# All weight splits on VectorE, loads of x and of running sums from GpSimd's queue, LoRA columns in two buffers, another order in the last unit: a fused dense and NF4 layer pair in float32

## The reference

```python
base  = einsum('bsi,oi->bso', x, weight) + bias1
low   = einsum('bsi,bri->bsr', x, lora_a[adapter])       # rank 16, one adapter per batch row
delta = einsum('bsr,bor->bso', low, lora_b[adapter])
h     = base + scale[adapter] * delta
w2    = NF4[codes] * absmax        # 64 elements to a block, 2048 x 2048
out   = x + (einsum('bsd,od->bso', h, w2) + bias2)
```

## Time and profile before

| | |
|---|---|
| time, median of 3 runs | 2107.86 us (2107.43 to 2111.29) |
| the profiled execution | 2105.49 us, its span 2103.7 us |
| TensorE busy | 96% of the span |
| VectorE busy | 77% |
| ScalarE busy | 42% |
| GpSimd busy | 6% |
| mean granted clock of TensorE | 0.985 |
| DMA | 526 MB, 250 GB/s over the span |

### The profile page before, as it was taken

How to read it: one execution, slowest core, us unless ns; L and a number is a source line. 1 busy time by engine, 2 the same in 40 slices (tenths; PEclk the granted TensorE clock), 3 DMA queues, 4 the chain that set the end, 5 groups by cost and what they waited for, 6 DMA issues and landing times.

```text
span 2103.7 us, 29439 instructions
## 1 busy us (share of the span) xinstructions
PE 2016.7 (96%) x10880; PEld 1713.2 (81%) x10880; DVE 1610.5 (77%) x2377; ACT 883.8 (42%) x1417; POOL 118.9 (6%) x79
## 2 busy tenths in 40 slices
PE   4899999999999999989999999989999999998997
PEld 4788778788878777889989989989997887886876
DVE  8899879866996465575577787787778778778887
ACT  8655555554555332343442342243242234234332
POOL 5100000000000000000020020020002002002000
PEclk8999999999999999999999999999999999999999
DMA  9778878887888788856478677786877878877876
GB/s 283 244 239 263 256 250 259 254 253 244 264 266 252 244 264 275 256 190 218 166 262 269 217 263 257 250 282 210 271 259 231 275 253 261 260 234 242 279 257 231
DMA packets 406277, 526.14 MB, mean 250 GB/s; under 512 B 22992, under 2 KB 293024, under 8 KB 406008
## 3 DMA queue, kind: packets, MB, share of 16 engines
q1 hardware_dynamic: 402824, 513.23, 75.6%
q0 software_dynamic: 3312, 11.03, 1.6%
HBM read 336.47 MB, written 188.76 MB: 250 GB/s over the span
## 4 chain that ended last, share of the span: by engine, by line
PE 80%; DVE 8%; DMA 5%; issue 3%; SPq 2%; ACT 1%; DVEq 0%; ACTq 0%
PE big L1638 19%; PE big L1640 19%; PE big L1639 19%; PE big L1826 10%; PE big L1824 10%; PE big L1653 2%; DVE comb L1324 2%; DMA rq<-xc_d 1%; PE big L1634 1%; DMA xc_d<-rq 1%; DMA a_br<-a_sel_d 1%; DMA comb_raw<-wc_d 1%; DVE r_sb L1452 1%; DMA code_w<-in_L_ffn_codes_dram 1%; DVE xs L1374 1%
## 5 line engine op out<-in xcount | busy, mean ns | idle before, releaser
L1824 PE MATMUL big<-comb,xs 128*128 128x256 f32 x1920 | 468.9, 282 | 15.0 <-DVE r_sb L1452 13.8
L1638 PE MATMUL big<-wq,tile 128*128 128x512 f32 x1088 | 468.4, 431 | 1.2 <-DVE tile L1259 1.2
L1826 PE MATMUL big<-comb,xs 128*128 128x272 f32 (+1 forms) x1920 | 468.0, 286 | 0.0
L1640 PE MATMUL big<-wq,tile 128*128 128x512 f32 x1088 | 427.2, 393 | 0.0
L1639 PE MATMUL big<-wq,tile 128*128 128x512 f32 x1088 | 426.3, 392 | 0.0
L1824 PEld LDWEIGHTS big<-comb,xs 128*128 128x128 f32 x1920 | 363.9, 190 | 20.1 <-DVE comb L1324 14.7
L1826 PEld LDWEIGHTS big<-comb,xs 128*128 128x128 f32 x1920 | 363.9, 190 | 2.3
L1638 PE MATMUL big<-comb,xs 128*128 128x512 f32 x832 | 332.3, 399 | 21.5 <-DVE r_sb L1452 14.8
L1452 DVE TENSOR_TENSOR r_sb<-big,r_sb 128x512 f32<-128x512 f32 x328 | 225.6, 688 | 149.7 <-PE big L1640 98.5
L1640 PE MATMUL big<-comb,xs 128*128 128x512 f32 x832 | 330.6, 397 | 0.0
L1639 PE MATMUL big<-comb,xs 128*128 128x512 f32 x832 | 330.4, 397 | 0.0
(11 more groups left out here) (144 smaller groups left out, 2440.7 us busy)
## 6 DMA issues: line engine op xcount, KB each, us to landing
raw<-in_L_cond_weight_dram SPq DMA_DIRECT2D x128, 512.0 KB, 4.5
xg<-xc_d SPq DMA_DIRECT2D x112, 512.0 KB, 5.3
xc_d<-rq SPq DMA_DIRECT2D x26, 1792.0 KB, 7.6
r_sb<-m_d SPq DMA_DIRECT2D x80, 512.0 KB, 4.9
m_d<-r_sb SPq DMA_DIRECT2D x64, 512.0 KB, 6.1
wc_d<-cs SPq DMA_DIRECT2D x31, 896.0 KB, 4.9
tb<-wc_d SPq DMA_DIRECT2D x107, 256.0 KB, 5.0
x_nat<-in_x_dram SPq DMA_DIRECT2D x104, 256.0 KB, 4.0
```

The costliest lines, as they stand in the source:

```text
L1638: nc.tensor.matmul(out_ap, t_hi, m_hi, start=first, stop=False, skip_group_check=onto)
L1640: return nc.tensor.matmul(out_ap, t_lo, m_hi, start=False, stop=last, skip_group_check=onto)
L1824: nc.tensor.matmul(big[:, bank, 0:HW], x, w[:, 0:HW], start=begin, stop=end, skip_group_check=not opens)
L1826: ins = nc.tensor.matmul(big[:, bank + 1, 0:wide], x, w[:, HW:HW + wide], start=begin, stop=end, skip_group_check=not opens)
```

## The change

- `BY_GPSIMD` goes. All 14 halves of every stage are split by VectorE. `LO_STEPS` gets the four: half 10 beside half 9 at step 8 (k = 1 of a stage's first unit), 11 at step 9 (k = 2), 12 at step 10 (k = 3), 13 at step 11 (k = 4).
- `load_x` and `load_base` move from SP to a loop on GpSimd: wait until all lower parts of unit u's x are made, load x of u + 1, then (for u + 1 in 8 to 47) wait for the store of the sum that used the buffer and load the running sum. The first x stays on SP with a semaphore of its own.
- `a_b` and `a_br` get a second buffer; `load_a(u + 2)` moves to the top of unit u (from u = 1 on) and waits for the placing of unit u's columns.
- In the last unit all four LoRA pairs are multiplied behind k = 3 and k = 4, those of the second block first; that block's totals are loaded ahead into the freed x buffer (`total_end`); the final additions are made in three parts of each block and each part is stored as it is done.

```diff
-    BY_GPSIMD, ON_VECTOR = (A12, A22), 10
     def half_at(i, f, c):
-        n = halves_of(i).index((f, c)) + 1
-        if i and f in BY_GPSIMD:
-            return 4 * (i - 1) + n - ON_VECTOR
-        return 2 * NF + ON_VECTOR * (i - 1) + n if i else n
+        return 2 * NF * i + halves_of(i).index((f, c)) + 1
-    LO_STEPS = {-1: [0], 0: [1], 2: [2], 3: [3], 5: [4], 6: [5, 6], 7: [7, 8], 8: [9]}
+    LO_STEPS = {-1: [0], 0: [1], 2: [2], 3: [3], 5: [4], 6: [5, 6], 7: [7, 8], 8: [9, 10], 9: [11], 10: [12], 11: [13]}
+    TAIL = ((0, slice(0, 2)), (1, slice(1, 2)), (1, slice(0, 1)))
+    def pair_at(u, n):
+        m, t = divmod(n, 2)
+        return (1 - m, t) if u == NU - 1 else (m, t)
+        total_end = at("total_end", 176, [P, 2, 2, SW], F32)
-        a_b = at("a_b", 59, [P, 2, 3, QT, R], F32R)
+        a_b = [at(f"a_b{i}", kb, [P, 2, 3, QT, R], F32R) for i, kb in enumerate((59, 57))]
...
@@ sync @@
             def load_a(u):
-                if u:
-                    sp.wait_ge(s_aside, len(WITH_LOW) * u)
+                if u >= 2:
+                    sp.wait_ge(s_aside, len(WITH_LOW) * (u - 1))
+                elif u:
+                    sp.wait_ge(s_btst, 16 * NS)
             for u in range(NU):
-                if u + 1 < NU:
-                    sp.wait_ge(s_xlo, NF * (u + 1))
-                    load_x(u + 1)
+                if u and u + 2 < LOWS:
+                    load_a(u + 2)
                 if 1 <= u <= BOTH:
                     store_sums(u - 1, 1)
+                if u == NU - 1:
+                    sp.wait_ge(s_xlo, NF * NU)
+                    for t in range(2):
+                        sp.dma_start(total_end[:, t, :, :].rearrange("p n o -> p (n o)"), m_d[3, q, :, t, :]
+                                     ).then_inc(s_tend, 16)
...
-                    if k == 1 and QB <= u + 1 < BOTH:
-                        load_base(u + 1)
...
-                if u + 2 < LOWS:
-                    load_a(u + 2)
+                if u == 0:
+                    load_a(2)
-            for m in range(2):
-                store_total(NU - 1, m)
+            for n, (t, cols) in enumerate(TAIL):
+                for m in range(2):
+                    sp.wait_ge(s_end, 2 * n + m + 1)
+                    src = (r_sb[(NU - 1) % 2] if m else total[(NU - 1) % 2])[:, t, cols, :]
+                    sp.dma_start(out_block(QB - 1, t, m, 1)[:, 2 * cols.start:2 * cols.stop, :],
+                                 src.rearrange("p n (c o) -> p (n c) o", c=2)).then_inc(s_out[m], 16)
@@ gpsimd @@
-            for i in range(1, NF):
-                for n in range(ON_VECTOR, 2 * NF):
-                    f, c = halves_of(i)[n]
-                    ks = slice(HALF * c, HALF * (c + 1))
-                    pool.wait_ge(s_chi, 2 * NF * i + n + 1)
-                    tt(cw[f][:, ks, LO, 0:SW], cr[f][:, ks, LO, 0:SW], cw[f][:, ks, HI, 0:SW].bitcast(F32),
-                       ALU.subtract).then_inc(s_clo_p, 1)
+            for u in range(NU):
+                if u + 1 < NU:
+                    pool.wait_ge(s_xlo, NF * (u + 1))
+                    load_x(u + 1)
+                if QB <= u + 1 < BOTH:
+                    load_base(u + 1)
@@ vector @@
+            def add_end(n):
+                u = NU - 1
+                t, cols = TAIL[n]
...
+                first, both, out = (b[:, t, cols, :] for b in (total[u % 2], total_end, r_sb[u % 2]))
+                tt(first, first, out, ALU.add).then_inc(s_end, 1)
+                dve.wait_ge(s_end, 2 * n + 1)
+                tt(out, both, out, ALU.add).then_inc(s_end, 1)
+                    if u == NU - 1 and k in (3, 4):
+                        for n in range(2 * (k - 3), 2 * (k - 2)):
+                            add_lora_pair(u, n)
+                    if u == NU - 1 and k == 5:
+                        add_end(0)
+                        add_end(1)
+                    if u == NU - 1 and k == 6:
+                        add_end(2)
@@ tensor @@
-                        for n in {3: (0,), 4: (1,), 6: (2, 3)}.get(k, ()):
+                        for n in ({3: (0, 1), 4: (2, 3)} if u == NU - 1 else {3: (0,), 4: (1,), 6: (2, 3)}).get(k, ()):
                             multiply_lora_pair(u, n)
```

More of the change, by code:

```diff
@@ L426, in adaln_ffn_kernel @@
         s_cpy = sem("product_copied")
-        s_ab = sem("a_b_loaded")
+        s_ab = [sem(f"a_b_loaded{i}") for i in range(2)]
         s_adf = sem("a_b_difference_made")
@@ L582, in load_last_b22, with load_first_x @@
                                      wc_d[2 + jj, OUTER[0], :, lo:hi, :]).then_inc(s_wl[B22], 16)
-            def load_x(u):
-                i, q = divmod(u, QB)
+            def load_first_x():
                 for t in range(2):
[L587 to L595, removed]
+                    sp.dma_start(xg[:, t, :, :, :].rearrange("p h k t -> p (h k) t"), xc_d[t, OUTER[0]]
+                                 ).then_inc(s_xg0, 16)
             def load_total(u, m):
@@ L840, in _, with load_x, load_base @@
                             load_low(u + 1, t, m)
-            for m in range(2):
-                store_total(NU - 1, m)
+            for n, (t, cols) in enumerate(TAIL):
[4 more added lines that the diff above has]
+                                 src.rearrange("p n (c o) -> p (n c) o", c=2)).then_inc(s_out[m], 16)
             for n in range(2):
                 sp.wait_ge(s_rst[n], 32 * (BOTH // 2))
-                sp.wait_ge(s_out[n], 32 * QB)
+                sp.wait_ge(s_out[n], 32 * (QB - 1) + 16 * len(TAIL))
         @block.gpsimd
         def _(pool):
+            def load_x(u):
+                i, q = divmod(u, QB)
+                for t in range(2):
+                    pool.dma_start(xg[:, t, :, :, :].rearrange("p h k t -> p (h k) t"), xc_d[2 * q + t, OUTER[i]]
+                                 ).then_inc(s_xg, 16)
+            def load_base(u):
+                i, q = divmod(u, QB)
+                pool.wait_ge(s_rst[u % 2], 32 * (u // 2))
+                for t in range(2):
+                    pool.dma_start(r_sb[u % 2][:, t, :, :].rearrange("p n o -> p (n o)"), m_d[BASE_OF[i], q, :, t, :]
+                                 ).then_inc(s_rld[u % 2], 16)
             def store_early(m):
@@ L1004, in x_hi @@
                 if f in (A11, A12, A22):
-                    act.wait_ge(s_xg, 32 * (u + 1))
+                    if u:
+                        act.wait_ge(s_xg, 32 * u)
+                    else:
+                        act.wait_ge(s_xg0, 32)
                     if f == A22 and u >= 2:
@@ L1376, in a_difference @@
             def a_difference(u):
-                dve.wait_ge(s_ab, 16 * (u + 1))
-                tt(a_br[:, LO, 2, :, :], a_br[:, LO, 1, :, :], a_br[:, LO, 0, :, :], ALU.subtract).then_inc(s_adf, 1)
+                low, high, apart = (a_br[u % 2][:, LO, h, :, :] for h in range(3))
+                dve.wait_ge(s_ab[u % 2], 16 * (u // 2 + 1))
+                tt(apart, high, low, ALU.subtract).then_inc(s_adf, 1)
             def a_lo(u):
                 dve.wait_ge(s_abhi, u + 1)
-                tt(a_b[:, LO, :, :, :], a_br[:, LO, :, :, :], a_b[:, HI, :, :, :].bitcast(F32),
+                tt(a_b[u % 2][:, LO, :, :, :], a_br[u % 2][:, LO, :, :, :], a_b[u % 2][:, HI, :, :, :].bitcast(F32),
                    ALU.subtract).then_inc(s_ablo, 1)
@@ L1790, in multiply @@
                 if q == 0:
-                    pe.wait_ge(s_clo_p if i and f in BY_GPSIMD else s_clo, max(half_at(i, f, c) for c in range(2)))
+                    pe.wait_ge(s_clo, max(half_at(i, f, c) for c in range(2)))
                 if u < LOWS and f in WITH_LOW:
```

46 lines of the change are left out of this document (31 added, 15 removed).

## The result

The changed kernel takes 2111.78 us in the median (2107.17 to 2120.0), the kernel before 2107.32 beside it (2103.47 to 2111.29). The ratio is 1.0022, 95% interval 1.0014 to 1.0029: 0.2% slower, where 0.13% faster was forecast. The profiled execution took 2110.96 us, span 2109.2, against 2105.49 and 2103.7 before.

What follows compares the result with a forecast made beforehand. TensorE was taken as the bound, VectorE in the first units of stages 1 to 6; 8.6 - 7.8 - 3.0 + 0.8 + 4.2 = 2.8 us faster, so 2105.1 us from 2107.86, range 2096 to 2113.

Steps and rivals of the forecast that it cites:

- Splits, stands: First units, stages 1 to 5: VectorE's chain 13.6 us, TensorE stands 4.0 to 4.6 before the seventh product; 8.6 gained.
- Clock: First units: the product after each new stand runs at a low clock, 7.8 us lost, bounds 0 and 10.
- Late upper part of A, 3.0: Units 8, 16, 24: ScalarE makes A's upper part 1.2 to 1.7 us after VectorE wants it; 3.0 lost.
- these three terms: First units of stages 1 to 5: splits 8.6 us gained, clock 7.8 lost, late upper part of A 3.0 lost.
- Unit 48: VectorE's 4.03 us wait for x goes, but x overtakes the S3 loads; +0.8 us, bounds -2 and +3.
- The overtaking: x in GpSimd's queue passes SP's weight loads, which can slip 2.7 us at a turn; 2.2 in unit 48.
- Last unit: Behind the last product only two 512-element additions and one 256 KB store; 4.2 us gained, bounds 3 and 5.3.
- Loads of x, the step that failed: x moves to GpSimd's queue: 3.0 us lost in units 8, 16 and 24, nothing in ordinary units.
- a lower bound of 4.3 us: Units 8, 16 and 24: x overtaking weight loads delays A's upper part, bounds 0 and -4.3 us, taken as -3.0.
- third rival, "weight loads crowded out": Last unit before and first of each stage: x and running sums delay weights, 11 us more, 2116 us; chance 0.15.
- "The running sums are issued at the same moment before and after.": Units around each stage's start: moving queues leaves the running sums' issue time unchanged; given against weight loads being crowded out.
- "They were not what VectorE waited for in stages 1 to 5.": First units of stages 1 to 5: VectorE did not wait for the loads of x; no size given.

Runs made afterwards that it cites:

- e4: Kernel before with only the new order of the last unit; 2104.2 us, ratio 0.9983.
- e6: Changed kernel with the loads of x back on SP, running sums staying on GpSimd; 2114.9 us, ratio 1.0034.
- e10: Changed kernel, last four splits earlier, x work of step 3 behind the fifth product's addition, x on SP, running sums on GpSimd; 2076.1 us, ratio 0.9858.
- e12: Changed kernel, last four splits earlier, x work of step 3 behind the fifth product's addition, both loads on GpSimd; 2085.0 us, ratio 0.9892.
- e1: Changed kernel with the loads of x and of the running sums back on SP; 2115.1 us, ratio 1.0032.
- e2: Kernel before with only the splits of A12 and A22 moved to VectorE; 2118.5 us, ratio 1.0053.
- e11: Changed kernel with the splits of A12 and A22 back on GpSimd, ahead of its running-sum loads; 2114.2 us, ratio 1.0032.
- e9: Changed kernel, last four splits earlier, x work of step 3 behind the fifth product's addition, both loads on SP; 2076.0 us, ratio 0.9848.
- e5: Changed kernel with the splits of A12 and A22 back on GpSimd, behind its running-sum loads; 2125.0 us, ratio 1.0081.
- e7: Changed kernel with the last four weight splits of each first unit earlier in VectorE's order; 2093.8 us, ratio 0.9928.
- e8: Changed kernel with the last four weight splits earlier and both loads on SP; 2088.8 us, ratio 0.9906.

## Why the prediction was wrong

- **Splits, stands.** Right in four units of five. The chain of 13.6 us (its terms as rounded give 13.4) was 13.37 in unit 8 up to the last split's start. From start to start, less the sixth product, the seventh came 4.3, 4.3, 4.4 and 4.0 us late in units 8, 16, 24 and 32 (3.99 in unit 8 is the last gap alone). In unit 40 it was 1.6 there; the greater stand was the 3.22 us for the LoRA transpose from SP, a path that the prediction did not have. In the other four kernels with both loads on GpSimd this transpose lands at 13.9 to 15.4 us after the unit's start, and in those with x on SP at 10.3 to 12.5.
- **Clock.** Right in kind and nearly in size: the products behind these stands took 1.4, 1.5, 2.3, 1.7 and 0.2 us more, 7.1 for the 7.8 booked; the fifth product of unit 40, behind the 3.22 us, took 0.9 more.
- **Late upper part of A, 3.0.** Too large. The wait was there, 0.85 us in unit 8 for the 1.2 to 1.7 expected, but VectorE stood for it in only two units, 1.7 us in sum. With these three terms the first five units were to be 2.2 us longer in sum; they are 0.5 shorter, within what such a sum varies.
- **Unit 48.** Forecast 0.8 gain, measured 1.9. The overtaking is there: the third product starts 1.5 us later in the unit than before, for the 2.2 booked.
- **Last unit.** Forecast 4.2 (bounds 3 and 5.3), measured 4.3, in the changed kernel and in e4.
- **Loads of x, the step that failed.** The prediction looked for the overtaking in the first units and in unit 48, with a lower bound of 4.3 us, and priced it in the last units of stages at nothing. There the weight blocks came late once x had GpSimd's queue, and the four units lost 10.1 us. This is the third rival, "weight loads crowded out", which got 0.15. Its place is only partly right (four turns and not six, and the first units no longer in sum). That its 11 us are so near is in part luck: 5.6 of the 10.1 are unit 31 of this one execution. Over all runs the sum of the four units is 87.0 to 92.2 us with both loads on GpSimd, the changed kernel's being the highest, and 80.9 to 82.1 with x on SP, so 5 to 7 us is the more usual price.
- **"The running sums are issued at the same moment before and after."** This is what spoke against that rival, and it was wrong in the changed kernel: they went out 1.2 to 2.4 us earlier in units 7, 15, 23 and 31. The prediction took x and the running sums one by one. It did not follow that x, once gone from SP's queue, lets the store of the old sum land sooner and so brings the next load forward, onto the weight block. That the move of x is needed for the loss is shown (e6 beside the changed kernel, e10 beside e12); that the earlier sums carry it is not.
- **"They were not what VectorE waited for in stages 1 to 5."** True of the kernel before, and no longer once VectorE has the splits: e1 stands 2.81 us for x in unit 32. The first units' forecast held only because x was early; with x on SP they are 9.1 us longer. The two parts of the change were costed as if apart. By themselves the splits cost 11 us (e2) and the queues with the splits on GpSimd some 10 (e11 against the 2104 of e4); together, 4.5 with the gain of the last unit inside.
- The Trainium skill's rule that was weighed (DMA: Bandwidth & Descriptors, section SWDGE vs HWDGE vs iDMA: the two kinds of queue are served in turn) was right to point at every turn. The trace agrees as far as that both kinds of queue moved data in the turn and SP's weights came late, though not in equal parts: 0.49 MB and 0.07 in the two us shown. What the sum lacked is not the lower bound in the first units but the unit before each turn.
- The difference that is left, 2.0 us in the profiled executions, is preparation (1.7 us longer, in a spread of 3.4 over all kernels) and ordinary units.

## What to carry to other kernels

When an engine becomes the bound of a stage, ask first in which order it does its work: two moves of work within VectorE's queue, first what TensorE wants next, then what frees its bank, and last what the next unit wants, gave 39 us (e1 to e9), where handing work or loads from one engine to another moved the time by 0 (e10) to 13 us (e5). When a load changes its queue, look at what is issued beside it for the whole stretch until both have landed, the unit before the stage included, ask which loads go out earlier because it is gone from its old queue, and lay the forecast of each part on the kernel with the other parts in it.

## What was not expected of the hardware

- A VectorE instruction of 512 elements took 10.31 us in e5, from 0.45 us before GpSimd's four splits began to 0.56 after they ended (9.30 us); the same in unit 16 (10.25 us). In the earlier trace rows such splits stretched VectorE's instructions to 2 to 3.4 us. There the four took 11.9 us and VectorE came between them.
- The loads of x land in 5.8 us in the median through GpSimd's queue and in 5.3 through SP's, a difference that says nothing of what comes of the move: the second half of a weight block came 1.7 us later in unit 23. From 10 to 12 us after the start of that unit GpSimd's queue moved seven times what SP's did. Which packets the block waits for is not settled. e6 and e10 show only that x in GpSimd's queue is needed for it, and that the running sums there, issued late, are not enough.
- Stands of up to 1.0 us before the seventh product, as in e9, left the clock at 1.00 in all five units. Of those of 1.8 to 2.2 us in e7 and e8 some were followed by a slow product (1.4 to 1.6 us more) and some by none, at the same length. In unit 31 of e11 even one of 3.2 us was followed by a product at a clock of 1.00.
